# A four-layer kernel: key stacks sent from GpSimd's queue, projections of the next block moved earlier

## The chip, the cores and the metric

The kernel runs on one core of one Trainium2 chip. A core has five engines that run their own instruction streams and meet at semaphores: TensorE (matmuls, into the eight banks of PSUM), VectorE, ScalarE, GpSimd, and SyncE, which here only issues transfers. The metric is the device time of one execution in microseconds; less is better.

## What is computed

Two pairs of an attention-like and a feed-forward layer, on x of 2 x 512 tokens by 512 channels. Each layer's input is layer-normalised, and its output is normalised and added:

```python
x = x + _layernorm(_L0_attn_ref(_layernorm(x), ...))   # a state-space layer, 64 heads
x = x + _layernorm(_L0_ffn_ref(_layernorm(x), ...))    # gated, ternary weights, 1792 hidden
x = x + _layernorm(_L1_attn_ref(_layernorm(x), ...))   # causal attention, 32 heads of 16
x = x + _layernorm(_L1_ffn_ref(_layernorm(x), ...))    # 8 experts, two per token
```

The change lies in the third:

```python
q = (x @ Wq.T + bq).reshape(b, l, h, hd).transpose(0, 2, 1, 3)
k = (x @ Wk.T + bk).reshape(b, l, h, hd).transpose(0, 2, 1, 3)
v = (x @ Wv.T + bv).reshape(b, l, h, hd).transpose(0, 2, 1, 3)
scores = jnp.einsum('bhqd,bhkd->bhqk', q, k) / math.sqrt(hd)
scores = jnp.where(causal, scores, -jnp.inf)
att = jax.nn.softmax(scores, axis=-1)
out = jnp.einsum('bhqk,bhkd->bhqd', att, v)
return out.transpose(0, 2, 1, 3).reshape(b, l, d) @ Wo.T + bo
```

## The kernel before

Every engine's program is written out by hand, in the order in which it runs; semaphores join them. The stages follow each other: the state-space layer up to about 1000 us of the span, the feed-forward layer to 1172, the attention layer to 1540, the experts to the end.

**Numbers in two parts.** Matmuls take rounded 32-bit operands, so each operand is kept as a high part (rounded by ScalarE) and a low part (the rest), and `products` (L365) issues three matmuls for each product of two: high by high, high by low, low by high. `low` (L370) is the subtraction that makes a low part, on VectorE or GpSimd.

**Before attention.** Eight tiles of 128 tokens go through the norms (`norm_turn` on TensorE transposes tile i, `norm_high` on ScalarE and `norm_low` on VectorE split it into `xTh`, `xTl`), and two tiles later TensorE multiplies a tile by the value weights (`values`, banks 2 and 3, 12 matmuls). In the program before, the queries' and keys' projections of the first block come after all eight value products.

**Projections.** A block m is one of 4 slices of 128 channels (8 heads) of one of 2 batches, so m = 0 to 7. `project(m, w, part)` adds the product of one of four slices of input channels, three matmuls of 512 columns, in bank 7; w = 0 are queries, w = 1 keys. When all four parts are in, ScalarE writes the high part `qh` out of the bank (`high`, L1147), VectorE the low part `ql` (`lows`, L1483), and only then may the bank be used for the next w. Before, `qh` and `ql` have one place for each w, and `high` of block m waits until both stacks of block m-1 have landed.

**Stacks.** A block makes two quads of 4 heads. For a quad, transfers build `qs` (queries, 6 transfers of 32 rows) and `kz` (keys, 12 of 16 rows, each pair of heads separated by zeros), with high and low parts one below the other, so that one matmul forms all three products of a score. There are two places, quad % 2; a place is free when the scores of the quad two before are done (`s_ready`). All 18 transfers of a quad are issued by SyncE (L590 queries, L595 keys).

**Units.** A quad is eight units, `unit(n)` = (quad, query tile, pair of heads), of growing width: 128, 128, 256, 256, 384, 384, 512, 512 keys. Unit n runs: scores on TensorE (L1896, and the mask L1897), maximum on VectorE (L1492), exponential on ScalarE (L1173); two units later its transposes on TensorE (L1907) and the copies out of the banks (ScalarE L1165, VectorE L1501). `weighted` (L1875) multiplies by the values in units 6 and 10 of a quad. `pieces(n)` says which part of which projection TensorE issues at the end of unit n. `weights(t)` on ScalarE (L1096, L1099) scales and rounds the raw query and key weights of slice t, and GpSimd makes their low parts `aql`; GpSimd also makes the low parts `awl` of the output weights, whose raw values `awr` lie in the place of `prob`, so the first exponential waits for them (`aw_lo`). Nothing else stands on GpSimd in this stage.

## Time and profile before

| | |
|---|---|
| median of three runs | 1714.3 us (1713.21 to 1725.72) |
| the profiled execution | 1710.41 us, span 1708.7 |
| TensorE matmuls busy | 1535.8 us (90% of the span) |
| VectorE busy | 1198.4 us (70%) |
| ScalarE busy | 809.2 us (47%) |
| GpSimd busy | 835.6 us (49%) |
| transfers issued by SyncE, share of the 16 engines' span | 17.5% |
| transfers issued by GpSimd | 2.1% |

The profile gives, for each instruction, its start and duration, the idle time of its engine in front of it, and the work whose end released it. TensorE's busy time is modelled, and its matmuls overlap by their pipelining; the spacing of the starts tells more than the durations. "PEclk" is the granted clock of TensorE as a share of full speed. The line numbers (L1896) are those of the kernel before.

### The profile page before, as it was taken

The numbers are of one execution on the slowest core, as the hardware profiler recorded it, in microseconds if no ns is written. First come the engines' busy times: TensorE is split into PE (matmuls) and PEld (weight loads), VectorE is DVE, ScalarE is ACT, GpSimd is POOL, SyncE is SP. The second block draws the span as 40 slices with busy tenths as digits, with TensorE's granted clock in tenths as the row PEclk, the third lists the DMA queues.
The fourth block names the chain that finished last, engine by engine and source line by source line (L and its number), as shares of the span: only waits on it lengthen the run. The fifth ranks groups of instructions, "written<-read, shape, count | busy, mean of one in ns | idle before, by whom it ended". The sixth has DMA issues, their size and how long they took to land.

```text
span 1708.7 us, 26177 instructions
## 1 busy us (share of the span) xinstructions
PE 1535.8 (90%) x8646; PEld 1197.6 (70%) x8646; DVE 1198.4 (70%) x2000; ACT 809.2 (47%) x1604; POOL 835.6 (49%) x761
## 2 busy tenths in 40 slices
PE   5899999999999999999999869996688888887796
PEld 3677877878778778777787658875565655666583
DVE  5777887788788787887787865657366666668524
ACT  3455555555545555555554423341266656564130
POOL 4377586676675766776766840007200000018454
PEclk9999999999999999999999889997899999997798
DMA  3111012021110110211101122120122111242344
GB/s 120 37 50 63 13 51 67 11 84 33 47 58 18 49 61 12 80 37 49 61 19 50 57 56 74 62 98 25 33 54 55 42 52 45 51 180 74 113 140 178
DMA packets 60249, 105.19 MB, mean 62 GB/s; under 512 B 12624, under 2 KB 37328, under 8 KB 54928
## 3 DMA queue, kind: packets, MB, share of 16 engines
q1 hardware_dynamic: 56496, 92.19, 17.5%
q0 software_dynamic: 3680, 12.06, 2.1%
q8 instruction: 42, 0.69, 0.2%
q14 instruction: 31, 0.25, 0.0%
HBM read 81.14 MB, written 10.49 MB: 54 GB/s over the span
## 4 chain that ended last, share of the span: by engine, by line
PE 57%; DVE 15%; POOL 8%; issue 7%; ACT 6%; DMA 4%; SPq 3%; POOLq 0%; DVEq 0%; ACTq 0%
PE banks L365 28%; PE banks L1653 6%; DVE tap L1235 4%; SPq L595 3%; PE banks L1907 3%; PE banks L1790 3%; PE banks L1718 2%; PE banks L1712 2%; PE banks L1683 2%; DMA x<-in_w_gate 2%; POOL wol L370 2%; PE banks L1875 2%; PE banks L1727 2%; PE banks L1896 2%; DVE nmax L1492 1%
## 5 line engine op out<-in xcount | busy, mean ns | idle before, releaser
L1235 DVE SCALAR_TENSOR_TENSOR tap<-banks,parg,tap 128x511 f32<-128x511 f32 (+2 forms) x288 | 215.1, 747 | 26.4 <-ACT tap L949 19.2
L755 POOL TENSOR_TENSOR am<-ah,upto 128x1024 fp32r<-128x1024 f32 x64 | 121.7, 1901 | 177.6 <-PE banks L1683 136.5
L365 PE MATMUL banks<-xTh,wch 128*128 128x512 f32 x384 | 162.2, 422 | 5.4 <-DVE em L1341 4.9
L957 ACT ACTIVATE th<-tap 128x512 f32<-128x512 f32 x96 | 60.7, 632 | 213.0 <-DVE tap L1235 211.0
L365 PE MATMUL banks<-xTh,wcl 128*128 128x512 f32 x384 | 151.0, 393 | 0.0
L365 PE MATMUL banks<-xTl,wch 128*128 128x512 f32 x384 | 150.1, 391 | 0.0
L1173 ACT ACTIVATE prob<-banks,nmax 128x128 f32<-128x128 f32 (+3 forms) x256 | 122.0, 526 | 59.1 <-DVE nmax L1492 58.2
L1492 DVE TENSOR_REDUCE nmax<-banks 128x2 f32<-128x256 f32 (+3 forms) x128 | 105.0, 820 | 55.8 <-PE banks L1897 55.8
L1907 PE MATMUL banks<-ident,prob 128*128 128x128 f32 x640 | 106.8, 296 | 18.5 <-DVE pB L1501 8.6
L755 POOL TENSOR_TENSOR am<-al,upto 128x1024 fp32r<-128x1024 f32 x64 | 122.1, 1908 | 0.0
L1341 DVE TENSOR_TENSOR em<-banks,gmask 128x1024 f32<-128x1024 f32 x64 | 78.2, 1222 | 50.3 <-ACT banks L998 49.5
L1896 PE MATMUL banks<-kz,qs 128*128 128x256 f32 (+2 forms) x192 | 76.0, 436 | 37.8 <-DMA kz<-ql 34.6
L365 PE MATMUL banks<-xTh,wgh 128*128 128x512 f32 x256 | 107.4, 420 | 0.9 <-DVE tap L1235 0.5
L370 POOL TENSOR_TENSOR aql<-aqr,aqh 128x512 fp32r<-128x512 f32 x8 | 10.0, 1275 | 190.1 <-ACT aqh L1099 190.1
L365 PE MATMUL banks<-woh,ynTh 128*128 128x512 f32 x256 | 102.8, 402 | 0.0
L365 PE MATMUL banks<-woh,ynTl 128*128 128x512 f32 x256 | 101.0, 394 | 0.0
L365 PE MATMUL banks<-xTh,wgl 128*128 128x512 f32 x256 | 100.8, 394 | 0.0
L365 PE MATMUL banks<-wol,ynTh 128*128 128x512 f32 x256 | 100.7, 393 | 0.0
L365 PE MATMUL banks<-xTl,wgh 128*128 128x512 f32 x256 | 100.1, 391 | 0.0
L1907 PEld LDWEIGHTS banks<-ident,prob 128*128 128x128 f32 x640 | 78.4, 153 | 27.4 <-DVE pB L1501 12.5
L365 PEld LDWEIGHTS banks<-xTh,wch 128*128 128x128 f32 x384 | 72.1, 188 | 34.1 <-DVE em L1341 11.2
L1653 PE MATMUL banks<-xTh,gu 128*128 128x512 f32 x224 | 89.9, 401 | 6.1 <-DVE hidf L1430 6.1
(284 smaller groups left out, 4245.6 us busy)
## 6 DMA issues: line engine op xcount, KB each, us to landing
x<-grownT SPq DMA_DIRECT2D x96, 128.0 KB, 4.7
x<-in_w_conv SPq DMA_DIRECT2D x7, 1536.0 KB, 6.6
x<-in_w_gate SPq DMA_DIRECT2D x8, 1024.0 KB, 5.0
x<-in_w_out SPq DMA_DIRECT2D x8, 1024.0 KB, 4.8
eraw<-in_expert_w SPq DMA_DIRECT2D x8, 1024.0 KB, 7.3
gur<-in_ff_gu SPq DMA_DIRECT2D x7, 1024.0 KB, 4.8
x<-in_hidden SPq DMA_DIRECT2D x16, 256.0 KB, 3.8
qs<-qh SPq DMA_DIRECT2D x64, 64.0 KB, 2.0
```

What stands on the lines that cost most here:

```text
L365: m = nc.tensor.matmul(o, a, b, start=first and n == 0, stop=last and n == len(terms) - 1)
L595: sp.dma_start(kz[at:at + HD, quad % 2, p2, j, :].bitcast(F32), part[row:row + HD, w, :].bitcast(F32)).then_inc(qk_in[quad % 2], 16)
L755: m = pool.tensor_tensor(am[:, part, :, :], a[:, i, :].bitcast(F32).unsqueeze(2).to_broadcast([P, HG, P]), upto[:, :].unsqueeze(1).to_broa ...
L957: nc.scalar.activation(th[:, :], tap[:, q % 2, :], ACT.Tanh).then_inc(tanh_ready, 1)
L1173: e = nc.scalar.activation(prob[:, n % 2, j, 0:kw], scores(n)[:, j, :], ACT.Exp, bias=nmax[:, n % 2, j:j + 1])
L1235: nc.vector.scalar_tensor_tensor(tap[:, q % 2, sh:L], bk(CONV_BANKS[q % 2])[:, 0:L - sh], parg[:, KC * q + k:KC * q + k + 1], tap[:, q % 2 ...
L1341: nc.vector.tensor_tensor(em[:, s % 2, :, :], decayed, gmask[:, :].unsqueeze(1).to_broadcast([P, HG, P]), ALU.mult).then_inc(m_ready, 1)
L1492: nc.vector.tensor_reduce(nmax[:, n % 2, :], scores(n), AX, ALU.max, negate=True).then_inc(max_ready, 1)
L1653: m = mat(bk(2 * w + ft), gu[:, k, ft, w, :], part[:, k, tok], start=(k == 0 and part is xTh), stop=(k == KT - 1 and part is xTl))
L1790: m = mat(bk(4 + i % 4), part[:, k, i * P:(i + 1) * P], dn[:, k, :], start=(k == 0 and part is hidh), stop=(k == 1 and part is hidl))
L1896: mat(o, qs[:, quad % 2, p2, qi * P:kw], kz[:, quad % 2, p2, heads[0]:heads[1], 0:kw], start=True, stop=False)
L1907: m = pe.transpose(bk(4 + j)[:, c * P:(c + 1) * P], prob[:, w % 2, j, c * P:(c + 1) * P], ident[:, :])
```

## The change

Five edits go together:

- `pieces`: the next block's queries in units 0 to 3 of a pair of quads (before 3 to 6), keys in units 4 to 7 (before 8 to 11);
- the first block's projections run between the value products of tiles 3 to 7, two parts behind each of values(3) to values(6);
- `qh` and `ql` have two places, by m % 2, and `high` of block m waits for the stacks of block m-2;
- the twelve key transfers of a quad are issued by GpSimd (`padded`), the six of the queries stay on SyncE, each kind with semaphores of its own;
- GpSimd makes the low parts of the next weights in front of the first key stack of blocks 1, 3 and 5, and ScalarE's `weights` follow unit 9 (before unit 14).

```diff
-            for w, at in ((0, (3, 4, 5, 6)), (1, (8, 9, 10, 11))):
+            for w, at in ((0, (0, 1, 2, 3)), (1, (4, 5, 6, 7))):
...
+                    sp.wait_ge(qk_l, 2 * m + 1)
                     for u in range(2):
                         quad = 2 * m + u
                         if quad >= 2:
                             sp.wait_ge(s_ready, 8 * (quad - 1))
...
+                        for p2 in range(2):
+                            row = 32 * (2 * u + p2)
+                            for r, part in enumerate((qh, ql, qh)):
+                                sp.dma_start(qs[32 * r:32 * r + 32, quad % 2, p2, :].bitcast(F32),
+                                             part[row:row + 32, m % 2, 0, :].bitcast(F32)).then_inc(q_in[quad % 2], 16)
...
+                def padded(quad):
+
+                    if quad >= 2:
+                        pool.wait_ge(s_ready, 8 * (quad - 1))
+                    for p2 in range(2):
+                        for r, part in enumerate((qh, qh, ql)):
+                            for j in range(2):
+                                row, at = 32 * (2 * (quad % 2) + p2) + HD * j, 32 * r + HD * j
+                                pool.dma_start(kz[at:at + HD, quad % 2, p2, j, :].bitcast(F32),
+                                               part[row:row + HD, quad // 2 % 2, 1, :].bitcast(F32)).then_inc(k_in[quad % 2], 16)
+
+                pool.wait_ge(qk_l, 2)
+                padded(0)
                 pool.wait_ge(sel_ready, SEL + 3)
                 for k in range(KT):
                     pool.wait_ge(aw_hi, KT + k + 1)
                     low(pool, awl[:, k, :], awr[:, k, :], awh[:, k, :]).then_inc(aw_lo, 1)
...
+                padded(1)
+                for m in range(1, AT * NB):
+                    t = m // NB + 1
+                    if m % NB == 1 and t < AT:
                         for w in range(2):
-                            pool.wait_ge(aq_hi, 2 * (n // 32 + 1) + w + 1)
+                            pool.wait_ge(aq_hi, 2 * t + w + 1)
                             low(pool, aql[:, w, :, :], aqr[:, w, :, :], aqh[:, w, :, :]).then_inc(aq_lo, 1)
+                    pool.wait_ge(qk_l, 2 * m + 2)
+                    for u in range(2):
+                        padded(2 * m + u)
...
-                        if n % 32 == 14 and n // 32 + 1 < AT:
+                        if n % 32 == 9 and n // 32 + 1 < AT:
                             weights(n // 32 + 1)
...
+                    if CH + 1 <= i <= NT:
+                        if i == CH + 1:
+                            pe.wait_ge(down_added, 4 + NT * FP)
+                        for part in (0, 1):
+                            project(0, (i - CH - 1) // 2, 2 * ((i - CH - 1) % 2) + part)
```

On GpSimd, from the clearing of the queries' fourth rows (`qs`) on, the program before has only the low parts of the output weights and of the three later pairs of weights:

```order
320 L883 MEMSET qs 32x2048 [waits sel_ready]
321 L370 TENSOR_TENSOR awl<-prob,awh 128x512 [waits aw_hi,sel_ready]
322 L370 TENSOR_TENSOR awl<-prob,awh 128x512 [waits aw_hi] x3
323 L370 TENSOR_TENSOR aql<-aqr,aqh 128x512 [waits aq_hi] x6
324 L370 TENSOR_TENSOR ewl<-eraw,ewh 128x512 [waits e_hi] x4
```

The changed program at the same place:

```order
320 L880 MEMSET qs 32x2048 [waits sel_ready]
321 L890 DMA kz<-qh 16x512 [waits qk_l]
322 L890 DMA kz<-qh 16x512 x3
323 L890 DMA kz<-ql 16x512 x2
324 L890 DMA kz<-qh 16x512 x4
325 L890 DMA kz<-ql 16x512 x2
326 L371 TENSOR_TENSOR awl<-prob,awh 128x512 [waits aw_hi,sel_ready]
327 L371 TENSOR_TENSOR awl<-prob,awh 128x512 [waits aw_hi] x3
328 L890 DMA kz<-qh 16x512 x4
329 L890 DMA kz<-ql 16x512 x2
330 L890 DMA kz<-qh 16x512 x4
331 L890 DMA kz<-ql 16x512 x2
332 L371 TENSOR_TENSOR aql<-aqr,aqh 128x512 [waits aq_hi] x2
333 L890 DMA kz<-qh 16x512 [waits s_ready,qk_l]
```

The first key stack's twelve issues now stand in front of the output weights' low parts, the second stack behind them, and the low parts of the second pair of weights in front of the stack of quad 2.

On TensorE, at the scores (`kz`, `qs`) of the first units of quad 0, the program before has two scores at once and the first piece of a projection (`xTh`, `aqh`) after unit 3:

```order
1830 L1896 MATMUL banks<-kz,qs 128x256 [waits qk_in0,sel_ready,v_f]
1831 L1897 MATMUL banks<-future,identb 128x256
1832 L1896 MATMUL banks<-kz,qs 128x256
1833 L1897 MATMUL banks<-future,identb 128x256
1834 L1896 MATMUL banks<-kz,qs 128x512 [waits exp_ready]
1835 L1897 MATMUL banks<-future,identb 128x2x128
1836 L1907 MATMUL banks<-ident,prob 128x128 [waits exp_ready]
1837 L1907 MATMUL banks<-ident,prob 128x128
```

The changed program:

```order
1830 L1924 MATMUL banks<-kz,qs 128x256 [waits q_in0,k_in0,sel_ready,v_f]
1831 L1925 MATMUL banks<-future,identb 128x256
1832 L366 MATMUL banks<-xTh,aqh 128x512 [waits qk_l]
1833 L366 MATMUL banks<-xTl,aqh 128x512
1834 L366 MATMUL banks<-xTh,aql 128x512
1835 L1924 MATMUL banks<-kz,qs 128x256
1836 L1925 MATMUL banks<-future,identb 128x256
1837 L366 MATMUL banks<-xTh,aqh 128x512
1838 L366 MATMUL banks<-xTl,aqh 128x512
1839 L366 MATMUL banks<-xTh,aql 128x512
```

A piece now follows every unit from unit 0 to unit 7 of an even quad, and none stands in an odd quad.

## Rows read from the trace of the kernel before

**Rows 1.** Waits, 1230 to 1535 us: who waited for whom, total, times, longest.
```profile
POOL aql L370 <- ACT aqh L1099: 190.1, 3, 73.7
...
PE banks L1896 <- DMA kz<-ql: 34.6, 8, 10.5
```

**Rows 2.** Timeline of TensorE, scores: start, duration, form, idle before and releaser.
```profile
1244.33 0.36 PE L1896 MATMUL banks<-kz,qs 128*128 128x256 f32 x1
...
1265.81 0.58 PE L1896 MATMUL banks<-kz,qs 128*128 128x256 f32 x1 [3.80 <-DMA kz<-ql]
...
1281.37 0.40 PE L1896 MATMUL banks<-kz,qs 128*128 128x512 f32 x1
...
1282.62 0.36 PE L1896 MATMUL banks<-kz,qs 128*128 128x256 f32 x1
...
1453.38 0.38 PE L1896 MATMUL banks<-kz,qs 128*128 128x256 f32 x1 [3.00 <-DMA kz<-ql]
...
1468.33 0.36 PE L1896 MATMUL banks<-kz,qs 128*128 128x256 f32 x1
...
1489.03 0.57 PE L1896 MATMUL banks<-kz,qs 128*128 128x256 f32 x1 [3.00 <-DMA kz<-ql]
...
1503.17 0.36 PE L1896 MATMUL banks<-kz,qs 128*128 128x256 f32 x1
...
1515.66 0.49 PE L1896 MATMUL banks<-kz,qs 128*128 128x512 f32 x1
```

**Rows 3.** Windows: stretch, length, busy PE, PEld, DVE, ACT, POOL, clock, transfers.
```profile
1489.00:1503.00 14.00, 13.74 (x114) 10.01 (x115) 9.25 (x18) 8.72 (x21) 0.00 (x0) 0.88 0.27 63
1503.00:1517.00 14.00, 13.28 (x120) 8.87 (x118) 10.90 (x20) 10.28 (x25) 0.00 (x0) 1.00 0.88 369
```

**Rows 4.** Transfers that write the key stacks, from issue to landing.
```profile
DMA to landing us min/median/max: 1.8/2.0/3.2
```

**Rows 5.** GpSimd's own issues, timeline, and the table of transfers (last number: landing).
```profile
1600.87 0.94 POOL L907 DMA_INDIRECT xg<-xnd,row_from  x1 [0.30 <-issue]
...
xg<-xnd,row_from POOLq DMA_INDIRECT x23, 3.6
```

**Rows 6.** Timeline of all engines, from the last value product to the first exponential.
```profile
1213.13 0.40 PE L365 MATMUL banks<-xTh,aqh 128*128 128x512 f32 x1
1213.37 0.39 PE L365 MATMUL banks<-xTl,aqh 128*128 128x512 f32 x1
1214.10 5.00 POOL L370 TENSOR_TENSOR awl<-prob,awh 128x512 fp32r<-128x512 f32 x4 [10.46 <-ACT awh L1139]
...
1221.49 0.75 DVE L1483 SCALAR_TENSOR_TENSOR ql<-banks,abqk,qh 128x512 fp32r<-128x512 f32 x1 [3.86 <-ACT qh L1147]
...
1222.27 2.40 SPq L595 DMA_DIRECT2D kz<-qh  x4
...
1231.22 0.55 PE L1896 MATMUL banks<-kz,qs 128*128 128x256 f32 x1 [10.49 <-DMA kz<-ql]
...
1232.57 1.14 ACT L1173 ACTIVATE prob<-banks,nmax 128x128 f32<-128x128 f32 x4 [11.12 <-DVE nmax L1492]
```

**Rows 7.** Timeline, the score and keys' evacuation of a unit of full width.
```profile
1278.37 0.40 PE L1896 MATMUL banks<-kz,qs 128*128 128x512 f32 x1
...
1281.65 0.69 ACT L1147 ACTIVATE qh<-banks,abqk 128x512 fp32r<-128x512 f32 x1
...
1282.37 0.75 DVE L1483 SCALAR_TENSOR_TENSOR ql<-banks,abqk,qh 128x512 fp32r<-128x512 f32 x1 [1.45 <-ACT qh L1147]
```

**Rows 8.** Timeline, unit 9's score and exponential; casting of the next weights.
```profile
1247.67 0.28 PE L1896 MATMUL banks<-kz,qs 128*128 128x256 f32 x1
...
1249.03 0.63 ACT L1173 ACTIVATE prob<-banks,nmax 128x128 f32<-128x128 f32 x2
...
1261.48 0.63 ACT L1096 ACTIVATE aqr<-aqr 128x512 f32<-128x512 f32 x1
1262.14 1.14 ACT L1099 CAST aqh<-aqr 128x512 fp32r<-128x512 f32 x2
```

More of the change, by code:

```diff
@@ L291, in program @@
         qk_ps, qk_h, qk_l, q_scaled = (sem(s) for s in ("qk_ps", "qk_h", "qk_l", "q_scaled"))
-        qk_in = [sem(f"qk_in{n}") for n in range(2)]
+        q_in = [sem(f"q_in{n}") for n in range(2)]
+        k_in = [sem(f"k_in{n}") for n in range(2)]
         s_ready, max_ready, exp_ready, pt_ps, pt_a, pt_v, pv_ps, o_out, o_tr, prec_ready, att_ready = (sem(s) for s in (
@@ L472, in program, with q_stacked, k_stacked @@
         SEL = 9 + 4 + 1
-        STACK = 2 * (3 + 3 * 2)
-        def stacked(quad):
-            return 16 * STACK * (quad // 2 + 1)
+        def q_stacked(quad):
+            return 16 * 6 * (quad // 2 + 1)
+        def k_stacked(quad):
+            return 16 * 12 * (quad // 2 + 1)
         def group_steps(eng, step):
@@ L1134, in _, with high @@
             if STAGES >= 3:
-                norm_scalar(2)
+                def high(m, w):
+                    act.wait_ge(qk_ps, 2 * m + w + 1)
+                    if m >= 2:
+                        for u in range(2):
+                            if w:
+                                act.wait_ge(k_in[u], k_stacked(2 * (m - 2) + u))
+                            else:
+                                act.wait_ge(q_in[u], q_stacked(2 * (m - 2) + u))
+                    nc.scalar.activation(qh[:, m % 2, w, :], bk(7), ACT.Identity,
+                                         bias=abqk[:, w, m // NB:m // NB + 1]).then_inc(qk_h, 1)
+                act.wait_ge(small_in, 16 * 12)
+                nc.scalar.activation(abqk[:, 0, :], abqk[:, 0, :], ACT.Copy, scale=HD ** -0.5).then_inc(q_scaled, 1)
+                act.wait_ge(q_scaled, 2)
+                for i in range(NT):
+                    norm_high(2, i)
+                    if i >= NT - 2:
+                        high(0, i - NT + 2)
                 act.wait_ge(v_ps, NT)
@@ L1473, in values, with lows, between @@
                                             abv[:, :].rearrange("p (h d) -> p h d", h=AH), ALU.add).then_inc(v_f, 1)
-                norm_vector(2, 3, lambda n: values(n - 6) if n >= 6 else None)
+                def lows(m, w):
+                    dve.wait_ge(qk_h, 2 * m + w + 1)
+                    nc.vector.scalar_tensor_tensor(ql[:, m % 2, w, :], bk(7), abqk[:, w, m // NB:m // NB + 1],
+                                                   qh[:, m % 2, w, :].bitcast(F32), ALU.add, ALU.subtract).then_inc(qk_l, 1)
+                def between(n):
+                    if n >= 6:
+                        values(n - 6)
+                    if n == NT + 2:
+                        lows(0, 0)
+                norm_vector(2, 3, between)
+                lows(0, 1)
                 for i in range(NT - 2, NT):
@@ L1478, in _ @@
             if STAGES >= 3:
-                def lows(m, w):
-                    dve.wait_ge(qk_h, 2 * m + w + 1)
-                    nc.vector.scalar_tensor_tensor(ql[:, w, :], bk(7), abqk[:, w, m // NB:m // NB + 1],
-                                                   qh[:, w, :].bitcast(F32), ALU.add, ALU.subtract).then_inc(qk_l, 1)
-                for w in range(2):
-                    lows(0, w)
                 for n in range(UNITS + O_BACK - 7):
@@ L1839, in values @@
                                              for k in range(KT)]).then_inc(v_ps, 1)
-                pe.wait_ge(aw_lo, KT)
-                pe.wait_ge(hid_f, 4 * FP)
-                for i in range(NT + 2):
-                    if i < NT:
-                        norm_turn(2, i)
-                    if i >= 2:
-                        values(i - 2)
                 def project(m, w, part):
@@ L1861, in project @@
                         o.then_inc(qk_ps, 1)
+                pe.wait_ge(aw_lo, KT)
+                pe.wait_ge(hid_f, 4 * FP)
+                for i in range(NT + 2):
+                    if i < NT:
+                        norm_turn(2, i)
+                    if i >= 2:
+                        values(i - 2)
+                    if CH + 1 <= i <= NT:
[3 more added lines that the diff above has]
+                            project(0, (i - CH - 1) // 2, 2 * ((i - CH - 1) % 2) + part)
                 def weighted(quad, hf):
@@ L1878, in weighted @@
                     m.then_inc(pv_ps, 1)
-                pe.wait_ge(sel_ready, SEL)
-                for w in range(2):
-                    for part in range(KT):
-                        project(0, w, part)
                 pe.wait_ge(v_f, NT)
@@ L1890, in _ @@
                         if n % 8 == 0:
-                            pe.wait_ge(qk_in[quad % 2], stacked(quad))
+                            pe.wait_ge(q_in[quad % 2], q_stacked(quad))
+                            pe.wait_ge(k_in[quad % 2], k_stacked(quad))
                         if n >= 2:
```

36 lines of the change are left out of this document (5 added, 31 removed).

## The prediction

> **What bounds the kernel now.** I read the waits of the attention stretch first, then the scores in the timeline, then what each score waited for. Over the whole span TensorE is busy 90% of the time (the table above), but the attention stretch, from 1230 us on, has one regular hole: TensorE waits for the key stack `kz`, 34.6 us in 8 times, while GpSimd idles 190.1 us in front of three pairs of weight halves [rows 1]. The hole is easy to place. The sixteen quads of eight units begin at known scores [rows 2]: quad 1 at 1244.33, quad 2 at 1265.81 after 3.80 us idle, quad 3 at 1282.62, quad 12 at 1453.38, 13 at 1468.33, 14 at 1489.03 after 3.00 us idle, 15 at 1503.17. So the wait stands before every even quad, seven times, besides the one before quad 0. The reason lies in the order of the work: both projections of the next block run in units 3 to 6 and 8 to 11 of a pair, so the keys' low half comes out of VectorE only after unit 11, and twelve transfers of SyncE's queue must still be issued and land before unit 16.
>
> The same rows give the prices of quads. Quad 12 (four pieces of projection, full clock) takes 1468.33 - 1453.38 = 14.95 us. Quad 13 (four pieces, and the delay that two evacuations `high` and `lows` put between exponential and the next maximum) takes 20.7 - 3.0 = 17.7 us. Quad 15 has no piece: its eighth unit begins 12.49 us after its first, and from an eighth unit to the next quad is 1.25 us (1281.37 to 1282.62), so some 13.8 us. A piece is three matmuls 0.234 us apart, 0.70 us [rows 6]; 14.95 less four pieces is 12.15 us of TensorE work in a quad.
>
> A hole also costs clock. Behind the stall of 3.0 us quad 14 ran at a granted clock of 0.88 and took 14.14 us, quad 15 at 1.00 took 13.8 [rows 3]: 0.3 to 0.4 us, part of the time at the lower of the two levels, 1.2 against 2.4 GHz. Quad 2, behind 3.80 us, took 16.81 us where quad 12 with the same work took 14.95: 1.9 us. Six pairs, quad 2 to 14, take 223.2 us: 6 x (14.95 + 17.7 + 3.5) = 216.9, and the other 6.3 is this clock loss. From unit 8 to quad 14 it is 1489.03 - 1244.33 = **244.7 us**.
>
> **What the new queue has to deliver.** Call c the spacing of two transfers issued by GpSimd and L the time from the last issue to its landing; a key stack takes 11c + L. On SyncE four issues take 2.40 us, with the gaps between groups c = 0.63, and L = 2.0 [rows 4, 6], so 9.0 us; the first stack indeed took from 1222.27 to 1231.2. No direct transfer stands on GpSimd's queue in this trace. The nearest rows are its gathers of 128 rows: 0.94 us with a gap of 0.30, so one each 1.25 us, landing after 3.6 us [rows 5]. A key transfer has 16 rows of 2 KB instead of 128, so I bound c below by SyncE's 0.63 and above by 1.25, L between 2.0 and 2.8 (longer than SyncE's, shorter than that of a gather eight times the size). The kind of queue is the gather's, the size is the SyncE transfer's, so I take the middle, c = 0.95 and L = 2.4: a stack is 12.85 us.
>
> The Trainium skill, DMA: Bandwidth & Descriptors, Latency and other measured facts, gives about 1 us to the first byte for transfers whose descriptors GpSimd computes in software, against about 0.6 us on SyncE's path; an estimate of c from it would be 1.0, and the sum below would be about 5 us higher. The trace shows 0.6 us an issue on SyncE and 0.94 plus a gap of 0.30 for a gather, so it agrees in direction.
>
> **The steady part.** The pieces of the next block now all lie in units 0 to 7, the even quad of a pair. Even quad: 12.15 + 8 x 0.70 = 17.75, and about 0.75 because the piece at unit 4 follows at once the one at unit 3, whose bank must first be evacuated by `high` and `lows` (0.69 + 0.75 us) [rows 7]: **18.5 us**. Odd quad: 13.8 and 0.6 for the second evacuation that falls on its first maxima: **14.4 us**. Together 32.9, against 32.65 before. So the move of the projections saves nothing by itself.
>
> How long has GpSimd for the stack of the next even quad? Its wait is the keys' low half, now after unit 7. In the rows of a unit of that size the score began at 1278.37 and `ql` ended at 1283.12, 4.75 us later; the next unit's score follows 1.25 us after the seventh's (1281.37 to 1282.62) plus a piece, so the low half is there 2.8 us into the odd quad [rows 2, 7]. That leaves 14.4 - 2.8, **about 11.5 us**, and the stack needs 12.85: a stall of 1.35. In three of the seven pairs GpSimd must first make the halves of the next weights: they wait for ScalarE, which casts them after unit 9. Unit 9's score is some 2.3 us into the quad, its exponential ends 2.0 later (at 1249.66 for the score at 1247.67), scale and first cast take 0.63 + 0.57, two lows at 1.25 us 2.5 [rows 6, 8]: 8.1 us into the quad, 5.3 later than the others. With about 1 us that the earlier casts add to that quad, the window is 7.2 us and the stall 5.65. What is queued behind the weights on GpSimd is just the stack TensorE waits for.
>
> Sum from unit 8 to quad 14, seven odd and six even quads: 7 x 14.4 + 6 x 18.5 + 3 x 1 = 214.8; stalls 4 x 1.35 + 3 x 5.65 = 22.4; clock loss 3 x 1.5 + 4 x 0.4 = 6.1 (between the 0.3 and 1.9 of above). That is 243.3 against 244.7: **-1.4 us**.
>
> The odd quads' stacks may start as soon as GpSimd is free and have 18.5 us for 12.85. Queries stay on SyncE, six transfers or 3.8 us. Both are hidden; without that cover each would show in full. SyncE's two weight loads wait behind queries only and land 3 us later, well ahead of unit 9 of the pair after. The expert loads need the last stack, some 4 us later than now, and the 1527 us where they are first used leaves over 10 us. Splitting `qh`, `ql` in two places costs nothing: the same instructions, less waiting.
>
> **The start.** Eight pieces (5.6 us) move between the value products, from tile 5 on, where TensorE is already the bound. All but the last value product and the projections end at 1213.1 - 2.8 + 5.6 = 1215.9; with 0.69 and 0.75 the keys' low half is there at 1217.5 instead of 1222.2 [rows 6]. The stack lands at 1217.5 + 12.85 = 1230.4 instead of 1231.2. But GpSimd now issues those twelve transfers before the four lows of the output weights, which stood at 1214.10 in the gap before, and ScalarE's first exponential waits for these lows, since `prob` lies on the raw weights. They end at 1217.5 + 11.4 + 5.0 = 1233.9, so the first exponential is 1.3 us late (1232.57 before). From it to unit 8 were 11.8 us; four more pieces, of which two lie under the wait, and the evacuation make it 14.2: unit 8 at 1248.1 instead of 1244.33. The stack of quad 1 comes at 1233.9 + 12.85 = 1246.8, in time. **+3.8 us.**
>
> Sum: +3.8 - 1.4 = **+2.4 us** on the profiled execution of 1710.41 us (span 1708.7), 1712.8. The median of the three runs, 1714.3, is 3.9 higher than the profiled one; I say 1713, no change that could be measured.
>
> **The bounds of c.** c = 0.63, L = 2.0: start 0; no stall in four pairs, 1.8 in three; 214.8 + 5.4 + 1.2 = 221.4, so -23 us. c = 0.8, L = 2.2: start +2.0, stalls 11.4, clock 3, so -13.5. c = 1.08, L = 2.5: start +5.5, stalls 33, clock 7, so +16. c = 1.25, L = 2.8: start +9.7 (quad 1's stack is late too), stalls 48.3, clock 10.5, so +39. A tenth of a microsecond in c is worth about 10 us.
>
> **Rivals.**
> 1. *Cheap issues.* c is below 0.8, so stacks hide but for the three pairs with weights: -13 to -23 us, about 1693. For it: only 16 rows, and a gather must also read its indices. Against: the fixed 0.30 gap between gathers. Chance 0.30.
> 2. *Dear issues, the slower side.* GpSimd's transfers cost what its gathers cost, from c = 1.08 on. The place is the same, TensorE's first score of every even quad: stalls of 5 and 9 us seven times, in place of 3.5, +16 to +39 us, about 1742. For it: the only rows on this queue. Against: they move eight times the bytes. Chance 0.23.
> 3. *The issues are held up by VectorE.* If an issue had to wait for VectorE's instruction in flight, 0.4 to 1.2 us of maxima and copies (one of them in [rows 7]), c would pass 1.25 and the loss 40 us. Against: in this stretch every VectorE instruction reads a bank, none copies from SBUF to SBUF. Chance 0.05. The Trainium skill, SBUF — State Buffer, Who interferes with whom, says that VectorE in its two-port modes locks GpSimd out of writing descriptors, which speaks against moving transfers to this queue; by the same section reductions and one-input instructions outside those modes don't take the lock. No row here shows a direct GpSimd transfer beside VectorE.
> 4. *The change does what it says and no more*, my forecast: stalls of 1 and 6 us in place of 3.5. Chance 0.42.
>
> **Numbers.** About 1% (17 us) is what a measurement can tell from no change. Faster by more than that is rival 1: 0.30. Within it the forecast: 0.42. Slower, rivals 2 and 3: 0.28. The range leaves out the outer end of rival 2 and rival 3: 1690 to 1745; the forecast's own range is 1701 to 1728.
>
> **What would show it.** In the profile of after: the spacing of `kz` issues on GpSimd (0.95; 0.8 or less is rival 1, 1.1 or more rival 2) and their landing. TensorE's waits at the scores by quad: about 6 us before quads 2, 6, 10 and 1 us before 4, 8, 12, 14. Quads of about 18.5 and 14.4 us. The first exponential near 1234, unit 8 near 1248. I am wrong if the stalls before quads 2, 6, 10 equal the others (then the weights aren't in the way), if even quads take under 17 us (pieces fill gaps I count as work), or if the keys' low half is much earlier than 2.8 us into the odd quad.

## The result and the profile after

The changed kernel takes **1689.0 us** (median of four runs, 1688.0 to 1690.6) against 1717.5 of the kernel before timed beside it; the ratio is 0.9849, 95% interval 0.9824 to 0.9874. It is 1.5% faster. The forecast was 1713, no change that could be measured; of its rivals, rival 1 (cheap issues, about 1693) comes nearest. The time lies 1 us below the low end of the range and 24 us below the forecast. The medians are 28.5 us apart, the two profiled executions, whose traces are read below, 19.8.

The profiled execution took 1690.6 us. Its page:

```profile
span 1688.6 us, 26177 instructions
PE 1534.2 (91%) x8646; PEld 1191.1 (71%) x8646; DVE 1196.5 (71%) x2000; ACT 806.9 (48%) x1604; POOL 927.8 (55%) x953
...
q1 hardware_dynamic: 50352, 85.88, 15.9%
q0 software_dynamic: 9824, 18.37, 3.9%
```

GpSimd has 192 more instructions than before, the key transfers. They are what to look at first: their duration, and how far apart they start. The line L890 by itself (ns min/median/max, first and last start), then GpSimd's timeline after an odd quad's key half, then the table of transfers (last number: us from issue to landing).

```profile
L890 POOL DMA_DIRECT2D kz<-qh x128: 484/484/780, 1220.3 to 1466.8; - x128
```
```profile
1282.56 1.91 POOL L890 DMA_DIRECT2D kz<-qh  x4 [16.51 <-DVE ql L1498]
1284.46 0.96 POOL L890 DMA_DIRECT2D kz<-ql  x2
1285.41 1.92 POOL L890 DMA_DIRECT2D kz<-qh  x4
1287.31 0.96 POOL L890 DMA_DIRECT2D kz<-ql  x2
```
```profile
kz<-qh POOLq DMA_DIRECT2D x128, 32.0 KB, 1.9
kz<-ql POOLq DMA_DIRECT2D x64, 32.0 KB, 1.8
```

Four issues take 1.91 us, and the next group follows without a gap: c = 0.475 us, L = 1.8. A key stack takes 11 x 0.475 + 1.8 = 7.0 us where the forecast had 12.85. It starts at 1282.56, 3.0 us into quad 3 (2.8 were forecast), and is whole at 1289.6, over 4 us before quad 4.

The waits, 1190 to 1515 us, which answer to [rows 1], and the scores at which quads 1, 2, 3, 4, 14 and 15 begin, which answer to [rows 2]:

```profile
POOL aql L371 <- ACT aqh L1115: 53.0, 3, 19.0
...
ACT prob L1193 <- POOL awl L371: 7.9, 1, 7.9
...
PE banks L1924 <- DMA kz<-ql: 6.5, 1, 6.5
...
PE banks L1924 <- issue: 4.3, 3, 2.3
```
```profile
1246.01 0.28 PE L1924 MATMUL banks<-kz,qs 128*128 128x256 f32 x1
...
1261.66 0.35 PE L1924 MATMUL banks<-kz,qs 128*128 128x256 f32 x1 [1.03 <-issue]
...
1279.55 0.28 PE L1924 MATMUL banks<-kz,qs 128*128 128x256 f32 x1
...
1293.91 0.36 PE L1924 MATMUL banks<-kz,qs 128*128 128x256 f32 x1
...
1462.60 0.36 PE L1924 MATMUL banks<-kz,qs 128*128 128x256 f32 x1
...
1476.44 0.36 PE L1924 MATMUL banks<-kz,qs 128*128 128x256 f32 x1
```

The 34.6 us in front of the key stacks are down to 6.5, the wait before quad 0 alone. Quad 3 takes 14.36 us, quad 15 is reached 13.84 us after 14. What is left are three waits of 1.0, 1.0 and 2.3 us before quads 2, 6 and 10, the pairs in which GpSimd makes the halves of the next weights first (the profile puts them down to "issue"; experiment 4 shows what they are). From quad 1 to quad 14 it is 1462.60 - 1246.01 = 216.6 us, against 244.7 before. In the windows of that stretch, before and after, TensorE's busy time falls by 6.4 us and the granted clock rises from 0.96 to 0.99: with the holes gone or short, the clock hardly falls to its lower level any more. Before, six of the seven even quads behind a stall of 3.0 to 3.9 us had a granted clock of 0.86 to 0.90 (quad 12 had 1.00); after, only quad 10 of this stretch, behind 2.3 us, is below 1.00 (0.91, and 19.5 us instead of 18.6).

```profile
1244.30:1489.00 244.70, 201.91 (x1667) 144.74 (x1665) 153.60 (x263) 151.14 (x337) 7.46 (x6) 0.96 0.19 47
```
```profile
1246.00:1462.60 216.60, 195.53 (x1653) 136.01 (x1652) 148.92 (x261) 146.86 (x334) 81.96 (x163) 0.99 0.23 53
```

**Where 8 us went back.** 28.1 us are gained there, but the span is only 20.1 us shorter. Quad 1 begins at 1246.01 instead of 1244.33, 1.7 us late. That lag is older than anything that the change touches: the transposes of tile 5 in the normalisation, before and after:

```profile
1197.75 0.66 PE L719 MATMUL banks<-ident,acc 128*128 128x128 f32 x4 [0.41 <-DVE acc L666]
```
```profile
1200.12 0.66 PE L716 MATMUL banks<-ident,acc 128*128 128x128 f32 x4 [0.39 <-DVE acc L663]
```

The code up to there is the same, and in the profiled executions of all fourteen kernels the same transposes start anywhere from 1194.6 to 1201.3. From there to quad 1 are 46.6 us before and 45.9 after, so beside the lag the start is 0.7 us shorter. (Experiment 7 shows that this is a gain and a loss together.) The larger part lies at the very end. GpSimd's last two adds in the kernel before (span 1708.7) and after (span 1688.6):

```profile
1702.12 2.48 POOL L707 TENSOR_TENSOR x<-x,acc 128x512 f32<-128x512 f32 x2
```
```profile
1676.15 2.48 POOL L704 TENSOR_TENSOR x<-x,acc 128x512 f32<-128x512 f32 x2
```

From their end to the end of the span are 4.1 us before and 10.0 after. The trace holds the reason in a record that the page's groups leave out: GpSimd's closing DRAIN instruction, the last long record of the span, starts at 1703.04 and takes 5.41 us before, at 1677.07 and 11.29 us after. Measured to the end of the last add, the work got 26.0 us shorter (1704.60 to 1678.63), and 5.9 us of it are given back by GpSimd's drain. Upstream +2.4, start -0.7, steady part -28.1, after quad 14 +0.4, drain +5.9: together -20.1.

### The profile page after: what moved, and what is told of

The parts are those of the page before. It is cut to its first block, busy times and chain, and to the rows that moved or that the text cites. A ratio compares the mean times of both kernels' runs of the same rounds, so it can differ in the third digit from the quotient of the medians.

```text
span 1688.6 us, 26177 instructions
## 1 busy us (share of the span) xinstructions
PE 1534.2 (91%) x8646; PEld 1191.1 (71%) x8646; DVE 1196.5 (71%) x2000; ACT 806.9 (48%) x1604; POOL 927.8 (55%) x953
## 4 chain that ended last, share of the span: by engine, by line
PE 59%; DVE 16%; POOL 8%; issue 7%; ACT 6%; DMA 3%; SPq 0%; POOLq 0%; DVEq 0%; ACTq 0%
PE banks L366 28%; PE banks L1679 6%; DVE tap L1255 4%; PE banks L1816 3%; PE banks L1935 3%; PE banks L1744 2%; PE banks L1906 2%; PE banks L1709 2%; PE banks L1738 2%; DMA x<-in_w_gate 2%; PE banks L1924 2%; POOL wol L371 2%; DVE nmax L1518 2%; PE banks L1753 2%; DVE xbc L1261 1%
## 5 line engine op out<-in xcount | busy, mean ns | idle before, releaser
L1193 ACT ACTIVATE prob<-banks,nmax 128x128 f32<-128x128 f32 (+3 forms) x256 | 121.8, 527 | 53.4 <-DVE nmax L1518 44.7
L890 POOL DMA_DIRECT2D kz<-qh x128 | 61.7, 490 | 104.8 <-DVE ql L1498 81.6
L1935 PE MATMUL banks<-ident,prob 128*128 128x128 f32 x640 | 100.0, 280 | 13.8 <-DVE pB L1527 7.2
L965 ACT ACTIVATE tap<-banks,parg 128x512 f32<-128x512 f32 x96 | 74.2, 773 | 43.6 <-PE banks L366 37.1
L1679 PE MATMUL banks<-xTl,gu 128*128 128x512 f32 x224 | 88.9, 397 | 0.0
```

The costliest lines, as they stand in the source:

```text
L890: pool.dma_start(kz[at:at + HD, quad % 2, p2, j, :].bitcast(F32), part[row:row + HD, quad // 2 % 2, 1, :].bitcast(F32)).then_inc(k_in[quad ...
L965: nc.scalar.activation(tap[:, q % 2, :], bk(CONV_BANKS[q % 2]), ACT.Identity, bias=parg[:, CT * KC + q:CT * KC + q + 1], scale=parg[:, KC ...
L1193: e = nc.scalar.activation(prob[:, n % 2, j, 0:kw], scores(n)[:, j, :], ACT.Exp, bias=nmax[:, n % 2, j:j + 1])
L1679: m = mat(bk(2 * w + ft), gu[:, k, ft, w, :], part[:, k, tok], start=(k == 0 and part is xTh), stop=(k == KT - 1 and part is xTl))
L1935: m = pe.transpose(bk(4 + j)[:, c * P:(c + 1) * P], prob[:, w % 2, j, c * P:(c + 1) * P], ident[:, :])
```

## The experiments

Twelve kernels bear on four questions: which of the edits brings the gain, whether the forecast's sum was right but for c, what the drain goes by, and whether the start matters. Ten stand in the table, two in experiment 10. The column "steady" is the time from quad 1's first score to quad 14's, "add" the end of GpSimd's last add, "drain" the duration of its closing instruction, all in us of the profiled execution (so "add" also carries how early or late that execution reached tile 5). Ratios are to the kernel before, on the same chip, with 95% intervals.

| kernel | median | ratio | steady | add | drain |
|---|---|---|---|---|---|
| before | 1712.0 to 1717.5 | 1 | 244.7 | 1704.6 | 5.41 |
| after | 1689.0 | 0.9849 (0.9824 to 0.9874) | 216.6 | 1678.6 | 11.29 |
| k1_keys_sync | 1679.7 | 0.9813 (0.9778 to 0.9848) | 211.9 | 1673.3 | 5.41 |
| k2_before_keys_pool | 1707.7 | 0.9971 (0.9954 to 0.9987) | 232.6 | 1692.8 | 11.29 |
| k3_late_pieces | 1704.3 | 0.9936 (0.9910 to 0.9962) | 233.4 | 1693.0 | 11.29 |
| k4_lows_between | 1684.8 | 0.9840 (0.9808 to 0.9872) | 211.9 | 1672.7 | 11.29 |
| k5_split8 | 1724.4 | 1.0078 (1.0061 to 1.0095) | 250.8 | 1716.3 | 7.37 |
| k9_sync_one_place | 1679.6 | 0.9815 (0.9797 to 0.9833) | 211.9 | 1673.5 | 5.41 |
| k10_sync_start_after | 1684.0 | 0.9851 (0.9829 to 0.9874) | 211.9 | 1672.9 | 5.41 |
| k11_sync_first_pool | 1681.8 | 0.9825 (0.9806 to 0.9844) | 211.9 | 1675.5 | 6.39 |
| k12_before_pieces_counts | 1683.2 | 0.9834 (0.9815 to 0.9854) | 212.0 | 1673.3 | 5.41 |
| k13_before_pieces | 1719.6 | 1.0029 (1.0017 to 1.0041) | 244.2 | 1715.6 | 5.41 |

**1. The keys back on SyncE's queue.**

```
-  pool.dma_start(kz[...], part[row:row + HD, quad // 2 % 2, 1, :]).then_inc(k_in[quad % 2], 16)
   # in SyncE's loop, behind the six transfers of the queries
+  sp.wait_ge(qk_l, 2 * m + 2)
+  sp.dma_start(kz[...], part[row:row + HD, m % 2, 1, :]).then_inc(k_in[quad % 2], 16)
```

> The changed kernel with the key transfers back on SyncE's queue, behind the queries' six of the same quad; projections, first projections and the two places stay as changed. Theory A (the second queue, whose key transfers go out every 0.475 us, brings the gain): the stack of 18 takes as long as before the change, and the time goes back to about 1710 to 1717 us. Theory B (the projections in units 0 to 7 bring it, by the arithmetic of windows): the key's low half is there 3.0 us into an odd quad, the queries' six issues lie before it, and 12 x 0.63 + 2.2 = 9.8 us later, 12.8 to 13.7 us into the quad, the stack is whole, under the 14.36 us of an odd quad; even quads of 18.5 us hide 18 x 0.63 + 2.2 = 13.5 us. No stall, about 1689 us or less. Theory C goes with B: the changed kernel's span runs on for 10.0 us after its last recorded GpSimd instruction where before's runs on for 4.1, because GpSimd ended with 238 transfers behind it instead of 46; here it would be 4.1 again and the time about 1683 us. If the longer end is chance, it stays at either value whatever the queue.

Measured: 1679.7 us, faster than the changed kernel, with which it shares everything but the queue: its slowest execution, 1684.4, is below the quickest of the changed kernel, 1688.0. B and C hold, A falls. SyncE's timeline in an odd quad that begins at 1278.37 (group by group, start and duration), and the score that opens the quad after it:

```profile
1280.65 0.51 SPq L592 DMA_DIRECT2D qs<-qh  x1
1281.21 2.48 SPq L599 DMA_DIRECT2D kz<-qh  x4
1283.73 1.22 SPq L599 DMA_DIRECT2D kz<-ql  x2
1285.00 2.49 SPq L599 DMA_DIRECT2D kz<-qh  x4
1287.53 1.22 SPq L599 DMA_DIRECT2D kz<-ql  x2
```
```profile
1292.74 0.36 PE L1915 MATMUL banks<-kz,qs 128*128 128x256 f32 x1
```

The queries are out before the key's low half is there; the last key transfer is issued at 1288.75 and needs about 2 us more, so the stack is whole some 2 us before it is read. The spacing is SyncE's old 0.63, and there is no wait. Over the steady part the granted clock is 1.00 (windows: stretch, length, busy PE, PEld, DVE, ACT, POOL, clock, transfers):

```profile
1245.40:1457.30 211.90, 194.46 (x1652) 134.62 (x1652) 148.61 (x261) 146.34 (x334) 7.56 (x6) 1.00 0.23 55
```

SyncE has nothing else to do here; GpSimd has (the weights' halves), and its queue costs the drain. The Trainium skill, DMA: Bandwidth & Descriptors, Issuing engines are not separate DMA queues, says that issuing from several engines saves only the time in which a sequencer issues, and this agrees: that time, 0.475 against 0.63 us a transfer, was covered.

**2. The queue alone**, in the kernel before (the low halves of weights placed between two key stacks, and queries and keys counted apart, since two engines now issue them; in the kernel before the joint count held nothing up: none of ScalarE's 14 high halves from 1230 to 1535 us waited).

```
-  sp.dma_start(kz[at:at + HD, quad % 2, p2, j, :], part[row:row + HD, w, :]).then_inc(qk_in[quad % 2], 16)
+  pool.dma_start(kz[at:at + HD, quad % 2, p2, j, :], part[row:row + HD, 1, :]).then_inc(k_in[quad % 2], 16)
```

> The kernel before with one thing of the change alone: the key transfers from GpSimd's queue (low halves of the next weights between the key stacks of a pair's two quads). Projections stay in units 3 to 6 and 8 to 11, parts in one place, the first projections behind the value products. Theory A (the queue brings the gain by itself): the key's low half comes about 7 us into an odd quad, 11 x 0.475 + 1.8 = 7.0 us later the stack is whole, at 14 us, and an odd quad with four of the eight pieces is 16.3 us long: no stall, so the attention is as short as in the changed kernel, 1689 to 1695 us. Theory B (the sooner projections are what does it): little is gained, 1708 us or more. Theory C on the end: 10 us after the last GpSimd add, as in the changed kernel.

Measured: 1707.7 us, a small gain: 7 us between the medians, 0.3% by the ratio (0.9971), and just under the 1708 of theory B. Odd quads take 19.2 to 21.9 us, not the 16.3 of expectation A. VectorE's key half, GpSimd's first group and the score that opens quad 6, in the pair whose odd quad begins at 1314.66:

```profile
1325.68 0.75 DVE L1498 SCALAR_TENSOR_TENSOR ql<-banks,abqk,qh 128x512 fp32r<-128x512 f32 x1 [1.29 <-ACT qh L1162]
```
```profile
1326.72 1.91 POOL L894 DMA_DIRECT2D kz<-qh  x4 [22.89 <-DVE ql L1498]
```
```profile
1334.56 0.36 PE L1912 MATMUL banks<-kz,qs 128*128 128x256 f32 x1 [2.20 <-issue]
```

The key's low half comes 11.8 us into the odd quad, not 7 as I had put down, and 8.1 us later the score starts, after a wait of 2.2. With pieces in units 8 to 11 not even the quick queue closes the hole; it saves 12.1 us in the steady part over seven pairs, and loses 5.9 at the end.

**3. The changed kernel with late projections.**

```
-  for w, at in ((0, (0, 1, 2, 3)), (1, (4, 5, 6, 7))):
+  for w, at in ((0, (3, 4, 5, 6)), (1, (8, 9, 10, 11))):
```

> The changed kernel with the projections of a pair back in units 3 to 6 and 8 to 11 (and the weights' rounding in unit 14), the low halves of the next weights between the two key stacks of a pair; the queue, the two places and the first projections stay changed. Theory A (queue): no stall, since 7 + 7.0 = 14 us is under the 16.3 us of an odd quad that holds four pieces: 1685 to 1691 us. Theory B (projections): at least 15 us are lost, above 1704 us.

Measured: 1704.3 us, and the same steady time as in experiment 2 within 1 us (233.4). Theory B, again. The two edits are now crossed: pieces late and SyncE 244.7 us, late and GpSimd 233, early and SyncE 211.9, early and GpSimd 211.9 (experiment 4). Once the pieces are early, the queue does nothing for the steady part. (The first of the four has the joint count; late pieces on SyncE with counts apart were not run.)

**4. The weights' halves between two stacks.**

```
   pool.wait_ge(qk_l, 2 * m + 2)
+  padded(2 * m)
   if m % NB == 1 and t < AT:   # aql, two low halves
       ...
-  for u in range(2):
-      padded(2 * m + u)
+  padded(2 * m + 1)
```

> The changed kernel, with GpSimd's low halves of the next weights between the key stacks of quads 2m and 2m + 1 instead of ahead of both. Theory A: they hold up the key stacks of quads 2, 6 and 10, which wait 1.0, 1.0 and 2.3 us on TensorE; moved behind these stacks they cost nothing, since quad 2m + 1's stack may only start once quad 2m's first scores are there: 3 to 5 us gained, 1684 to 1686 us, and quads 2, 6 and 10 come 14.4 us after 1, 5 and 9. Rival: the copies only take the place of another wait (the rounded weights come late on ScalarE anyway), less than 1.5 us gained, 1688 to 1689 us.

Measured: 1684.8 us, and the steady part falls from 216.6 to 211.9. Theory A: the three waits before quads 2, 6 and 10 were the two `aql` instructions in front of a stack on an in-order engine. GpSimd's timeline around the first of them, which in the changed kernel made these halves at 1252.03 and issued the stack from 1254.50 on:

```profile
1250.15 1.91 POOL L890 DMA_DIRECT2D kz<-qh  x4
1252.06 0.96 POOL L890 DMA_DIRECT2D kz<-ql  x2
1253.03 2.53 POOL L371 TENSOR_TENSOR aql<-aqr,aqh 128x512 fp32r<-128x512 f32 x2
1258.53 1.96 POOL L890 DMA_DIRECT2D kz<-qh  x4 [2.97 <-PE banks L1925]
```

The halves now lie in a gap in which GpSimd would wait for scores anyway.

**5. The forecast's own c.** Every key transfer is cut in two of 8 rows.

```
-  for j in range(2):      # 16 rows each
+  for j in range(4):      # 8 rows each
```

> The changed kernel with every key transfer cut in two of 8 rows: 24 issues from GpSimd for a quad's stack instead of 12, the same bytes. If an issue costs what it does whatever its rows, the twelve pieces go out every 0.95 us, which is the spacing that the forecast of 1713.0 us took: stack 23 x 0.475 + 1.8 = 12.7 us. Theory A (the forecast's sum was right but for the spacing): key low half 3.0 us into the odd quad, stack whole at 15.7 us against 14.36 us, so about 1.35 us more in the plain pairs and 5.6 us in the three with weights; the start 5.2 us later, and the clock falling in the stalls; the last recorded GpSimd add some 20 to 26 us later than in the changed kernel. Theory C (what the closing instruction of GpSimd costs goes by its transfers): 384 + 46 of them instead of 238, so 9.7 + 192 x 0.031 = 15.6 us after the last add: 1713 to 1722 us in all. Rival to C (it goes by bytes or packets): 9.7 us as in the changed kernel, 1708 to 1716. Rival to A (an issue of half the rows costs half): 1689 us, 1695 with C.

Measured: 1724.4 us, above the 1713 to 1722 expected. Line L890 over 1200 to 1512 us, and the waits before quads 4 and 6:

```profile
L890 POOL DMA_DIRECT2D kz<-qh x256 | 131.7, 523 | 61.5 <-DVE ql L1498 61.3 <-issue 0.2
```
```profile
1309.05 0.36 PE L1924 MATMUL banks<-kz,qs 128*128 128x256 f32 x1 [2.24 <-issue]
...
1349.13 0.55 PE L1924 MATMUL banks<-kz,qs 128*128 128x256 f32 x1 [7.59 <-issue]
```

An issue of 8 rows costs 0.51 us, one of 16 rows 0.475: halving the rows saves nothing. Twelve pairs of them are spaced c = 1.02, and a stack is 23 x 0.51 + 1.8 = 13.5 us. The forecast's rule of 10 us for each 0.1 of c gives 1713 + 7 = 1720 there; with the 2 us by which the drain grew, 1722. Measured 1724.4. The waits it named, 1.35 and 5.65, are 2.2 and 7.6 with a stack 0.7 us longer than its own. Against the kernel before on the same chip the change is +12.4 us, and the sum of the forecast with these two corrections is +2.4 + 7 + 2 = +11.4. So the sum was sound and c was wrong. The expectation of 26 us at most on the last add was short: it came 37.6 us later, since behind such waits even quads grew too, by up to 2.4 us, at a lower granted clock (0.957 over the span, 0.964 in the changed kernel).

**6. One place for the halves.** `qh` and `ql` indexed by 0 instead of `m % 2`, waits on the pair before instead of two before, on top of experiment 1.

> The kernel with the keys back on SyncE's queue (1679.7 us), and one place for qh and ql instead of two in turn. Theory A (with separate counts for queries and keys, two places hide nothing more): the next pair's queries' high half, in unit 3 and some 6 us into an even quad, waits for six issues that began with the quad, 5 x 0.63 + 2.2 = 5.4 us; the keys', in unit 7 and some 15 us into it, for a stack that ends at 17 x 0.63 + 2.2 = 12.9 us. 0 to 2 us more, 1680 to 1682. Rival (the places are needed): each even quad grows by 2 us or more, 1694 us or more.

Measured: 1679.6 against 1679.7 us, steady 211.9 in both. Theory A: the second place hides nothing.

**7. The first projections behind the value products**, on top of experiment 1 (ScalarE's and VectorE's halves of the first pair move behind their loops too).

```
-  for part in (0, 1):
-      project(0, (i - CH - 1) // 2, 2 * ((i - CH - 1) % 2) + part)
+  for w in range(2):          # behind the loop
+      for part in range(KT):
+          project(0, w, part)
```

> The kernel with the keys on SyncE's queue (1679.7 us), and the first pair's projections back behind the value products, with the rounding of the fourth weight ahead of the first halves on ScalarE, as in the kernel before. Theory A (the forecast's: the earlier start brings nothing, since the second value weight's halves hold the first exponential anyway, 1231.3 us with the changed order and 1232.6 in the kernel before, and the eight pieces only change places): within 1.5 us, 1679 to 1681. Rival: the start as changed is worth the five microseconds by which the key's low half comes sooner: 1684 to 1686 us.

Measured: 1684.0 us, 4 us more than in experiment 6 on the same chip (1679.6). At first sight the profiled execution speaks for theory A: quad 1 begins at 1244.87 against 1245.45 in experiment 1, and the last add ends at 1672.9 against 1673.3. But this execution, the quickest of four (1678.7 to 1689.3), was ahead before the edit could act. The transposes of tile 5, the same mark as above, and quad 1's first score, in experiment 1 and here:

```profile
1201.04 0.66 PE L724 MATMUL banks<-ident,acc 128*128 128x128 f32 x4 [0.41 <-DVE acc L671]
...
1245.45 0.28 PE L1915 MATMUL banks<-kz,qs 128*128 128x256 f32 x1
```
```profile
1194.62 0.66 PE L724 MATMUL banks<-ident,acc 128*128 128x128 f32 x4 [0.40 <-DVE acc L671]
...
1244.87 0.28 PE L1914 MATMUL banks<-kz,qs 128*128 128x256 f32 x1
```

From one to the other are 44.4 us with the changed start and 50.2 with the old one. The other kernels with early pieces say the same: with the changed start 44.6 in experiment 6, 44.4 in experiment 4 and 45.9 in the changed kernel (whose quad 0 had a granted clock of 0.78, against 0.87 in experiment 4), with the old start 50.2 in k12. Of the 5.8 us, 4.6 are there when quad 0's first score starts. So the rival holds: with early pieces the changed start is worth about 5 us, and the median of 1684.0 is the rival's. (The median alone would not show it: the intervals of this ratio and of experiment 6's touch.) With late pieces it is worth less: 43.1 us in experiment 3 against 46.3 in experiment 2 and 46.6 in the kernel before. The early pieces lengthen the old start by 3.6 us, and the changed start takes that back and more.

**8. Only quad 0's keys from GpSimd**, and the low halves of the fourth weight from VectorE, on top of experiment 1.

> The kernel with the keys on SyncE's queue (1679.7 us), but the twelve key transfers of quad 0 alone from GpSimd's queue, and the four low halves that GpSimd made there (4.92 us, ending 1227.8) from VectorE, which is idle for 7.8 us at that point. First scores 1229.8 -> about 1227.7 us (12 issues at 0.475 + 1.8 behind a key low half at 1220.2), the first exponential no longer behind the low halves: 2 us gained. Against it theory C: 12 transfers more for GpSimd's closing instruction, 12 x 0.031 = 0.4 us. 1678 us; if the start is held elsewhere, 1680.

Measured: 1681.8 us, no gain. Counted from the transposes of tile 5 (1201.29 here, 1201.04 in experiment 1), the first score comes 0.95 us sooner and quad 1 0.6 us, not 2, and the drain takes 0.98 us more. The last add also ends 2.2 us later than in experiment 1, all of it behind quad 14; as that stretch took 218.3 us in experiment 6 too, against 215.9 in experiment 1, this is not laid to the edit.

**9. What is needed of the change.** The kernel before with pieces in units 0 to 7 (and the weights' rounding in unit 9), once with queries and keys counted by two semaphores, once without.

```
-  for w, at in ((0, (3, 4, 5, 6)), (1, (8, 9, 10, 11))):
+  for w, at in ((0, (0, 1, 2, 3)), (1, (4, 5, 6, 7))):
   # k12 besides:
-  act.wait_ge(qk_in[u], stacked(2 * (m - 1) + u))
+  act.wait_ge(k_in[u] if w else q_in[u], ...)
```

> The kernel before with two edits alone: a pair's projections in units 0 to 3 and 4 to 7 (the next weights' rounding in unit 9), and the transfers of queries and of keys counted apart. All transfers on SyncE's queue, one place for the halves, the first projections behind the value products. Theory A (the gain is in the moved projections; everything else of the change brings nothing or costs): even quads 18.6 us, odd 14.4, no stall, 1679 to 1682 us. Rival (something else of the change is needed too): 1688 us or more.

> The kernel before with the moved projections alone, queries and keys still counted as one stack. The next pair's queries' high half then waits on ScalarE, some 6 us into an even quad, for all 18 transfers of the odd quad's stack, which began with the even quad and end 17 x 0.63 + 2.2 = 12.9 us into it; exponentials are queued behind it. Theory A: some 6 us in each of the seven even quads that have projections, less what TensorE makes up, 25 to 42 us over the kernel with separate counts: 1705 to 1722 us. Rival (the wait is covered, separate counts bring nothing): 1679 to 1683 us.

Measured: 1683.2 us with two counts, 1719.6 with one. Steady 212.0 and 244.2. Two edits of a few lines give what the whole change gives, and by the medians 6 us more (the two ratios, 0.9834 and 0.9849, have intervals that overlap). The traces show what this is made of: 5.9 us less drain, 4.6 less in the steady part, 4.3 more in the old start. The early pieces without separate counts give nothing (1.0029, slightly slower). What stands in the way in k13 is on ScalarE, here in the even quad that began at 1269.69:

```profile
1278.46 0.84 ACT L1173 ACTIVATE prob<-banks,nmax 128x256 f32<-128x256 f32 x2 [0.35 <-DVE nmax L1492]
1282.99 0.69 ACT L1147 ACTIVATE qh<-banks,abqk 128x512 fp32r<-128x512 f32 x1 [3.69 <-DMA kz<-ql]
```

The queries' high half waits 3.7 us for key transfers, of the next quad's stack, that it has nothing to do with, only because they count on the same semaphore; exponentials are queued behind it, and the even quad takes 23.9 us instead of 18.6.

**10. What the drain goes by.** In experiment 6's kernel GpSimd makes 60, then 120 transfers more into a tile that nobody reads.

> The kernel with the keys on SyncE's queue and one place for the halves (1679.6 us, 46 GpSimd transfers, closing instruction of GpSimd 5.41 us), with 60 transfers of 16 rows more from GpSimd, early in the attention, into a tile that nobody reads, in batches of twelve that it waits for; GpSimd is idle there. So far the closing instruction took 5.41 us with 46 transfers, 6.39 with 58, 11.29 with 238, and 7.37 with 430 of which 384 have 8 rows: steps of 0.98. Theory C1 (0.98 us for each twelve of 16 rows, beginning again after some number): 5.41 + 5 x 0.98 = 10.3 us. Theory C2 (0.031 us a transfer, the 58 and the 430 apart): 7.3 us. The attention itself is as short as without them.

> As the run before with 120 transfers more instead of 60. Theory C1: if it begins again after ten steps, as 192 more with 6 steps and 384 with 2 would fit, the closing instruction takes 5.41 us again; if it does not begin again, 15.2 us. Theory C2: 9.1 us.

The single times (1696.5 and 1731.6 us) mean nothing: the weights' halves are queued behind the batches on GpSimd and TensorE waits for them, 12.8 and 53.4 us in one quad, which the expectation had overlooked. The drains, from the trace's records of all kernels:

| transfers beyond the 46 gathers and scatters | 0 | 12 | 60 | 120 | 192 | 384 (8 rows) |
|---|---|---|---|---|---|---|
| drain, us | 5.41 | 6.39 | 10.31 | 5.41 | 11.29 | 7.37 |
| 5.41 + 0.98 x ((n / 12) mod 10) | 5.41 | 6.39 | 10.31 | 5.41 | 11.29 | 7.37 |

C1 holds in both: 10.3 and 5.41 were its forecasts (the other four values were known when the rule was made). Theory C as I first had it (0.031 us a transfer without end, 15.6 us in experiment 5) falls: it measured 7.37. All six values fit a drain that grows by 0.98 us for twelve transfers and begins again after 120. It does not go by bytes: 8 rows count like 16. Numbers that are no multiple of 12 were not tried, and why it begins again no run shows.

## Why the prediction was wrong

1. **The size that failed: c.** "I bound c below by SyncE's 0.63 and above by 1.25 ... so I take the middle." It is 0.475, below the lower bound, and L is 1.8, below 2.0, so a stack takes 7.0 us and not 12.85, and the stalls of 22.4 us that the sum counted came to 4.3. No row gave a reason that GpSimd could not issue faster than SyncE; the bound was a neighbour's price taken for a floor, and the direction that the forecast read from the trace, GpSimd the slower of the two, is the wrong one for these transfers. The gather was no guide either: its 0.94 us and gap of 0.30 belong to 128 rows with indices [rows 5].
2. **The arithmetic behind it held.** Even quads 18.5 (18.6 behind no wait, 17.9 behind the waits of 1.0 us, 19.5 behind the one of 2.3), odd quads 14.4 (14.36), key half 2.8 us into the odd quad (3.0): as forecast. Of the waits, only the order came true, longer where weights are in the way: 1.0, 1.0 and 2.3 us instead of 5.65, and none instead of 1.35 elsewhere. Experiment 5 puts the forecast's c into the kernel and finds its time within 3 us. With c = 0.475 it would have said 7.0 us of stack in windows of 11.5 and 7.2, and no wait.
3. **The window of 7.2 us in the three pairs with weights was too large.** GpSimd's stack began at 1254.50, 8.5 us into the quad (8.1 forecast), but the quad is 14.4 us, not 15.4: the 1 us added for the earlier casts is not there. 5.9 us for 7.0 gives the 1 us wait that stands before quad 2.
4. **"So the move of the projections saves nothing by itself" was the wrong conclusion.** The work of a pair stays 32.9 us, true, but the keys' half moves from 11.8 to 3.0 us into the odd quad, and that, with the counts apart, was worth all 33 us of the steady part (k12). The forecast had the sum at hand: under "The bounds of c" it puts SyncE's own prices, c = 0.63 and L = 2.0, into the new window and gets no stall in four pairs and -23 us. It read this as a case of a quick GpSimd, and not as what the moved projections give with the keys left where they were.
5. **The start**: +3.8 was forecast, -0.7 measured beside the lag from upstream. With c = 0.475 the twelve issues before the `awl` halves take 6 us instead of 11.4, these end at 1231.35, and the first exponential starts there and not at 1233.9. The moved first projections, which the forecast took for no gain, are worth about 5 us once the pieces are early (experiment 7).
6. **"Splitting `qh`, `ql` in two places costs nothing"**: right, and it brings nothing (experiment 6). What came with it, separate counts, is worth 36 us (k12 against k13). The forecast did not see that.
7. **Not foreseen:** the end of the program. Moving 192 transfers to GpSimd added 5.9 us to its closing drain. Without it the measured time would have been about 1683, an estimate from these two numbers, and 7 us outside the range; that the time fell so near the range's low end is luck.
8. **Rival 3**, issues held up by VectorE, did not show: the shortest and the median issue are both 0.484 us, the longest 0.78, beside a VectorE busy for 69% of the stretch.

## What to carry to other kernels

When a buffer's refill is late, look first at what releases it and when; a producer moved forward by four units removed a wait that a queue 25% quicker could not. A semaphore that counts two streams makes each wait for both: split the count before moving the producer. And price an untried operation with an interval that is open where no row closes it, in particular not by a neighbour's price as its floor; then run each edit of a bundle alone, for here two of five carried the gain, a third added about 5 us, one brought nothing and one cost 6 us. And before two profiled executions are compared at a late mark, compare them at one that the edit can't have moved: here they were up to 6.7 us apart there.

## What the hardware showed unexpectedly

- A direct transfer of 16 rows from tile to tile is issued by GpSimd every 0.475 us, back to back, and lands 1.8 us after its issue; SyncE issues the same every 0.63 and lands it in 2.0. Eight rows cost 0.51: fewer rows are no cheaper to issue.
- GpSimd's closing drain took 5.41 to 11.29 us, the same to 0.01 us in every kernel with the same number of transfers, and its six values fit 0.98 us for twelve, beginning again after 120. It lies at the end of the span, where nothing hides it.
- With no hole before a quad, the steady part took 211.9 or 212.0 us in six kernels, with a granted clock of 1.00 in each of them; in the kernel before it was 0.96.
